# Finding the tokens of each expert block: scattered copies in DRAM, or an inverted slot list and gathers, in a two-layer Mamba and mixture-of-experts kernel

## The reference, cut to what matters

```python
xn = layernorm(x)
# layer 0: selective scan over the 256 positions of a sequence, 16 states per channel
A_bar = exp(delta * A);  Bx = delta * x * B_sel
h_t = A_bar_t * h_{t-1} + Bx_t;  y = sum_n C_n * h_n + D * x
x = x + scan(xn) + moe(xn)
xn = layernorm(x)
# layer 1: heads of 8 channels, softmax of keys and queries
tran_V = softmax(K)^T outer V, summed over the heads;  out = softmax(Q) @ tran_V
x = x + heads(xn) + layernorm_affine(xn) + moe(layernorm_affine(xn))
# moe: 8 experts, the best 2 of each token
w, i = top_k(softmax(x @ gate), 2);  out = sum_k w_k * (gelu(x @ W1[i_k] + b1) @ W2[i_k] + b2)
```

## Time and profile before

| | us |
|---|---|
| median of 3 runs | 1062.06 |
| profiled execution, own time | 1060.0 |
| its span | 1058.3 |
| routing of layer 0 done | 116.7 |
| layer 0 scan groups | 118.9 to 537.1 |
| routing of layer 1 done | 637.0 |
| layer 1 heads done | 1035.4 |

### The profile page before, as it was taken

How to read it: one execution, slowest core, us unless ns; L and a number is a source line. 1 busy time by engine, 2 the same in 40 slices (tenths; PEclk the granted TensorE clock), 3 DMA queues, 4 the chain that set the end, 5 groups by cost and what they waited for, 6 DMA issues and landing times.

```text
span 1058.3 us, 17046 instructions
## 1 busy us (share of the span) xinstructions
PE 690.6 (65%) x4452; PEld 432.3 (41%) x4452; DVE 840.0 (79%) x1702; ACT 528.6 (50%) x1217; POOL 386.3 (36%) x358
## 2 busy tenths in 40 slices
PE   1883467399888988898921543233687786869670
PEld 0331122155545554455501442122565564747450
DVE  4898999699999999989967765814776859495968
ACT  2566533258676767666503611002565667465630
POOL 1565477613131313121201546773223232323320
PEclk9856598899998989898975555766696988889785
DMA  8369911101010101010050001111011111111108
GB/s 245 99 126 160 152 53 50 52 22 42 21 41 20 39 21 39 17 36 19 27 148 23 1 0 44 45 50 38 26 34 32 33 35 30 30 35 37 33 15 238
DMA packets 80124, 58.47 MB, mean 55 GB/s; under 512 B 9922, under 2 KB 71816, under 8 KB 80036
## 3 DMA queue, kind: packets, MB, share of 16 engines
q1 hardware_dynamic: 67108, 38.42, 17.1%
q0 software_dynamic: 8704, 16.87, 5.1%
q10 hardware_dynamic: 4224, 2.10, 0.7%
HBM read 28.89 MB, written 29.50 MB: 55 GB/s over the span
## 4 chain that ended last, share of the span: by engine, by line
DVE 35%; PE 20%; POOL 13%; ACT 12%; issue 11%; DMA 8%; SPq 1%; ACTq 0%; DVEq 0%; POOLq 0%
POOL slots L425 13%; ACT decay L521 5%; DVE decay L1231 4%; DVE work L1082 4%; DMA results<-res,xrow 4%; DVE hid_l L1045 4%; PE pb L827 3%; DVE x L970 3%; DVE work L1224 3%; DMA xrow<-slots 2%; DVE work L1091 2%; PE py L709 2%; PE po L749 2%; ACT hid L533 2%; DVE res L1050 2%
## 5 line engine op out<-in xcount | busy, mean ns | idle before, releaser
L431 POOL DMA_INDIRECT results<-res,xrow x144 | 164.2, 1140 | 469.3 <-DVE res L1050 455.6
L1082 DVE TENSOR_TENSOR_SCAN work<-decay,work 128x256 f32<-128x256 f32 x256 | 162.8, 679 | 1.1
L425 POOL DMA_INDIRECT slots<-rows,slot x128 | 136.7, 1068 | 72.2 <-issue 36.0
L533 ACT ACTIVATE hid<-ph,b 128x128 f32<-128x128 f32 x432 | 123.5, 369 | 69.3 <-PE ph L734 60.4
L709 PE MATMUL py<-work,idf 128*128 128x512 f32 x256 | 141.4, 641 | 1.1 <-DVE work L1091 1.0
L525 ACT COPY xrT<-px 128x256 f16<-128x256 f16 x144 | 53.4, 371 | 150.0 <-PE px L717 149.8
L749 PE MATMUL po<-w,hid_h 128*128 x576 | 124.4, 296 | 0.0
L690 PE MATMUL pb<-parts,pick 96*128 96x512 bf16 x256 | 86.3, 419 | 45.2 <-DVE work L1091 22.9
L748 PE MATMUL po<-w,hid_l 128*128 x576 | 115.5, 235 | 0.0
L1050 DVE TENSOR_REDUCE res<-po 128x128 f32<-128x256 f32 x144 | 59.5, 413 | 67.5 <-PE po L749 67.2
L1045 DVE TENSOR_TENSOR hid_l<-hid,hid_h 128x512 f16<-128x512 f32 x144 | 98.8, 686 | 17.0 <-ACT hid_h L539 16.8
(11 more groups left out here) (189 smaller groups left out, 1428.7 us busy)
## 6 DMA issues: line engine op xcount, KB each, us to landing
slots<-xrow SPq DMA_DIRECT2D x2, 4644.0 KB, 50.3
xrow<-slots SPq DMA_DIRECT2D x144, 64.5 KB, 1.9
decay<-in_w SPq DMA_DIRECT2D x32, 256.0 KB, 3.2
decay<-results SPq DMA_DIRECT2D x16, 256.0 KB, 4.2
big<-results SPq DMA_DIRECT2D x16, 256.0 KB, 4.7
results<-res,xrow POOLq DMA_INDIRECT x144, 2.3
x<-in_x SPq DMA_DIRECT2D x4, 512.0 KB, 6.4
slots<-rows,slot POOLq DMA_INDIRECT x128, 2.4
```

The costliest lines, as they stand in the source:

```text
L425: e.indirect_dma_start(slots_dram[l], bass.IndirectOffsetOnAxis(slot[:, k, t:t + 1], 0), rows[:, t, :], None).then_inc(s_disp[l][i], 16)
L431: e.indirect_dma_start(res_dram[l], bass.IndirectOffsetOnAxis(ids_of(j % XR), 0), res[:, j % XR, :], None, bounds_check=NRES - 1, oob_is_e ...
L533: ins = e.activation(hid[:, j % 2, c * P:(c + 1) * P], hidden(l, j)[:, c * P:(c + 1) * P], ACT.Gelu, bias=b1[:, col(en * HC + (l * NE * HC ...
L1082: ins = e.tensor_tensor_scan(work[:, 2 + n % 2, sl], decay[:, n, sl], work[:, n % 2, sl], 0.0, ALU.mult, ALU.add)
```

## The change

The slots are not filled by scattering rows any more. The rows (now 512 bytes, no number in them) are written to `rows_dram` in token order, group by group, by SyncE. On chip the list "slot of each pair" is turned into "pair of each slot". For each of 64 columns of pairs, VectorE makes a one-hot row of the low 7 bits of the slot (`lows`, 128 wide), and GpSimd one of the block number, times 128 (q + 1), and the same one-hot times the row number (`high_one`, `high_row`, 72 wide). PE multiplies them, 128 matmuls into one bank, and `rows_at` makes `pair_of` (for the scatter of results) and `row_of` (for the gather). Eight chunks of eight columns, two buffers each. Then GpSimd fetches each block's rows with an indirect DMA, four blocks ahead of its sends, and sends the results as before.

In layer 0 `lows` lies in group 0's scan loop after `scan(n)` for n = 0, 1, 3, 4, 6, 7, 9, 10, `invert` on PE two ticks later, and `rows_at` and `b2_in` at n = 14. In layer 1 all of it is in a row, `lows` inside `route` ahead of the weights of the choices. Blocks: layer 0 has 0, 10, 10, 10, 10, 10, 11, 11 ticks in its groups and a drain after the last scan; layer 1 has 9 in each of its 8 groups, with two quarters of `head_sum` at tick 7 and two at tick 8, and its products at ticks 5 and 6. The tick count runs on over group borders. The experts' numbers are read into registers nine at a time, not one per block. The sums over the heads are now turned when they are scaled (`t_` is written with a stride and read without one). The buffers of the hidden layer and of the one-hots share one arena.

```diff
-BPG = BLOCKS // (GROUPS - FIRST)
-ROWF = 2 * D + 2
+TICKS = ((0, 10, 10, 10, 10, 10, 11, 11), (9,) * GROUPS)
+ROWF = 2 * D
+AHEAD = 4
+CHUNK = 8
 @@ sync
-            e.wait_ge(s_const, 1)
-            for l in range(2):
-                e.dma_start(slots_dram[l].rearrange(...), fill[:, :]...).then_inc(s_zeroed[l], 16)
-                for i in range(DISP):
-                    e.wait_ge(s_disp[l][i], 16 * 2 * TILES // DISP)
+                for g in range(GROUPS):
+                    e.wait_ge(s_rlo, l * GROUPS + g + 1)
+                    e.dma_start(rows_dram[l][g * GC:(g + 1) * GC, :].rearrange("(t p) c -> p t c", p=P),
+                                rows[:, g * TG:(g + 1) * TG, :]).then_inc(s_rout, 16)
+                e.wait_ge(s_rout, 16 * GROUPS * (l + 1))
                 e.dma_start(b2, a[f"b2_{l}"]).then_inc(s_b2, 16)
-                for g in range(FIRST + 1, GROUPS):
-                    for j in range(BPG):
-                        block_rows(g, j, True)
 @@ gpsimd, after s_slot
-                            e.indirect_dma_start(slots_dram[l], bass.IndirectOffsetOnAxis(slot[:, k, t:t + 1], 0),
-                                                 rows[:, t, :], None).then_inc(s_disp[l][i], 16)
+                for c in range(CHUNKS):
+                    if c >= 2:
+                        e.wait_ge(s_inv, l * CHUNKS + c - 1)
+                    for i in range(CHUNK):
+                        q = c * CHUNK + i
+                        ins = e.tensor_scalar(high_one[:, c % 2, i, :], count_h[:, 0:BLOCKS], at_f[:, 1, q:q + 1],
+                                              float(P * (q + 1)), ALU.is_equal, ALU.mult)
+                    st.seq(ins)
+                    e.tensor_scalar(high_row[:, c % 2, :, :]..., high_one[:, c % 2, :, :]..., 0.0, row_f[:, 0:1],
+                                    ALU.is_gt, ALU.mult).then_inc(s_high1, 1)
+                def fetch(b):
+                    at = l * BLOCKS + b
+                    if at >= XR:
+                        e.wait_ge(s_xr, at - XR + 1)
+                    e.indirect_dma_start(xrow[:, b % XR, :], None, rows_dram[l],
+                                         bass.IndirectOffsetOnAxis(row_of[:, b:b + 1], 0)).then_inc(s_row[b % XR], 16)
+                for b in range(AHEAD):
+                    fetch(b)
+                for b in range(BLOCKS):
+                    if b + AHEAD < BLOCKS:
+                        fetch(b + AHEAD)
+                    send(b)
 @@ tensor
+            def invert(l, c):
+                e.wait_ge(s_low1, l * CHUNKS + c + 1)
+                e.wait_ge(s_high1, l * CHUNKS + c + 1)
+                for i in range(CHUNK):
+                    e.matmul(po[:, 0:BLOCKS], low_one[:, c % 2, i, :], high_one[:, c % 2, i, :], ...)
+                    ins = e.matmul(po[:, 0:BLOCKS], low_one[:, c % 2, i, :], high_row[:, c % 2, i, :], ...)
+                ins.then_inc(s_inv, 1)
 @@ tensor, last group of layer 0
+                if g == GROUPS - 1:
+                    for tick in range(BLOCKS, BLOCKS + DRAIN):
+                        blocks_tick(0, tick, expert)
                     to_tokens(g)
 @@ vector
+            def lows(l, c):
+                if c >= 2:
+                    e.wait_ge(s_inv, l * CHUNKS + c - 1)
+                for i in range(CHUNK):
+                    q = c * CHUNK + i
+                    ins = e.tensor_scalar(low_one[:, c % 2, i, :], count_h[:, :], at_f[:, 0, q:q + 1], None,
+                                          ALU.is_equal)
+                ins.then_inc(s_low1, 1)
+            def rows_at(l):
+                e.wait_ge(s_inv, (l + 1) * CHUNKS)
+                ...
+                e.tensor_scalar(row_of[:, :], pair_of[:, :], NTOK - 1, None, ALU.bitwise_and).then_inc(s_idx, 1)
-                    e.tensor_tensor(t_[:, 0:TG * HD * HD].rearrange("p (c d) -> p c d", d=HD), ...)
+                    e.tensor_tensor(t_[:, 0:TG * HD * HD].rearrange("p (t c d) -> p t d c", t=TG, d=HD), ...)
-                    tt = t_[:, t * HD * HD:(t + 1) * HD * HD].rearrange("p (d c) -> p c d", d=HD)\
+                    tt = t_[:, t * HD * HD:(t + 1) * HD * HD].rearrange("p (c d) -> p c d", d=HD)\
```

More of the change, by code:

```diff
@@ L43 @@
 HR = 3
-DISP = 4
 XIN = 4
 XR = 6
-assert BLOCKS >= 2 * TILES + NE - 1 and BPG % XR == 0 and BPG + DRAIN - 1 <= NS
+AHEAD = 4
+PAIRS = 2 * TILES
+CHUNK = 8
+CHUNKS = PAIRS // CHUNK
+BATCH = 9
+assert BLOCKS >= 2 * TILES + NE - 1 and all(sum(t) == BLOCKS for t in TICKS) and BLOCKS % BATCH == 0
 class Steps:
     def __init__(self, eng, sem):
-        self.eng, self.sem, self.n, self.off = eng, sem, 0, 0
+        self.eng, self.sem, self.n = eng, sem, 0
     def done(self, ins):
@@ L66, in seq @@
         self.wait()
[L68 to L82, removed]
 def build(nc, a, out):
@@ L98, in dram @@
             return nc.dram_tensor(name, shape, dt, kind="Internal").ap()
[L101 removed]
+        rows_dram = [dram(f"rows{l}", [NTOK, ROWF], F16) for l in range(2)]
         NRES = 2 * NTOK
@@ L764, in to_tokens, with scan_group @@
                 ins.then_inc(s_yTT, 1)
-            def scan_group(g, first=False, last=False, with_blocks=True):
+            def scan_group(g, expert):
+                ticks = ticks_of(0, g)
                 for n in range(NS):
@@ L771, in scan_group @@
                         b_row(g, n + 2)
-                    elif not last:
+                    elif g + 1 < GROUPS:
                         b_row(g + 1, n + 2 - NS)
-                    if with_blocks:
-                        blocks_at(0, g, n)
+                    if g == 0:
+                        for c in range(CHUNKS):
+                            if inverted_at(c) == n:
+                                invert(0, c)
+                    if n == 0 and g == 1:
+                        e.wait_ge(s_b2p, 1)
+                    if n < len(ticks):
+                        blocks_tick(0, ticks[n], expert)
                     if n >= 2:
                         y_sum(g, n - 2)
-                    if n == 0 and not first:
+                    if n == 0 and g > 0:
                         to_tokens(g - 1)
@@ L950, in route @@
                 e.tensor_scalar(eid[:, :], hit[0:1, :], float(NE - 1), None, ALU.min).then_inc(s_slot, 1)
+                for c in range(CHUNKS if l else 0):
+                    lows(l, c)
                 e.wait_ge(s_expout, l + 1)
@@ L1108, in scan_group @@
                     scan(g, n)
-                    if with_blocks:
-                        blocks_at(0, g, n)
+                    if g == 0:
+                        for c in range(CHUNKS):
+                            if inverted_at(c) == n + 2:
+                                lows(0, c)
+                        if n == NS - 2:
+                            rows_at(0)
+                            b2_in(0)
+                    if n < len(ticks):
+                        blocks_tick(0, ticks[n])
                     if n >= 1:
                         weigh(g, n - 1)
-                    if n == 1 and not first:
+                    if n == 1 and g > 0:
                         end_scan(g - 1)
                 weigh(g, NS - 1)
-                if not last:
+                if g + 1 < GROUPS:
                     begin_scan(g + 1)
@@ L1175, in _ @@
             route(1)
+            rows_at(1)
+            b2_in(1)
             q_, k_, v_, t_, o_ = (work[:, i, :] for i in range(5))
```

388 lines of the change are left out of this document (186 added, 202 removed).

## The result

The changed kernel takes 1259.78 us (median of 4 runs, 1254.39 to 1264.63) where the kernel before takes 1062.3 on the same chip (1061.4 to 1063.25): a ratio of 1.186, interval 1.181 to 1.191. Slower was forecast, but by 16 us; it is 197. The span of the profiled execution went from 1058.3 to 1252.6 us.

| stretch | before | after | difference | forecast |
|---|---|---|---|---|
| start to `eid` of layer 0 | 116.5 | 117.2 | +0.7 | +0.6 |
| group 0 | 39.0 | 70.4 | +31.4 | +20.4 |
| groups 1 to 7 | 377.0 | 446.3 | +69.3 | +1.0 |
| end of the last scan to `combine` | 9.2 | 16.8 | +7.5 | +6.0 |
| `combine` to `eid` of layer 1 | 92.7 | 93.3 | +0.6 | 0 |

A forecast was written before the change was run, and what follows sets the result against it. VectorE bounds layer 0; in layer 1 VectorE and PE take turns. Group 0 +20.4, groups 1 to 7 +1.0, layer 0's end +6.0, layer 1 -10.7: +16.7 on 1060.0, 1076.7, stated as 1078; range 1046 to 1110.

The forecast's parts named there:

- the late rows: Block ticks: PE waits for gathered rows, 28 us in layer 0's groups 1 to 7, 2.5 us a period in layer 1.
- GpSimd's one-hots: Layer 1's inversion: 2.8 us a chunk plus 0.3; as a rival 5 us a chunk, 1097 in all, chance 0.08.
- the register reads: Path from turn to `block_split`: 0.5 us taken off because the register load is done nine at a time.
- The loop of 11.3 us per three ticks: Layer 0's ticks: row fetch through out takes 11.3 us against 9.9, losing 1.4 three times a ten-tick group.
- the path of the row: Layer 0's ticks, from the end of out through send and gather to the row's landing: 4.5 us.
- The first rival: Rows come in time: gather lands in 2.0 us or less, layer 0 loses 6 us rather than 28; 1042, chance 0.22.
- the meetings: Waits for GpSimd's small instructions: 5 us for 28 in group 0, 0.3 us a chunk in layer 1.
- Group 0's work on VectorE: Layer 0's group 0: 64 one-hots at 0.20 us, 12.8 in all, `rows_at` 0.7 and `b2_in` 1.9.
- The shared way to SBUF: Rival, VectorE's one-hots beside GpSimd: all or half wait, 0.93 us each, +40 or +20; 1098 to 1118, chance 0.12.
- The end of layer 0: The blocks' drain behind the last scan delays the load of results: +6.0 us, bounds +3 and +9.
- the rival on it: Layer 1: the turned `t_` does not make L1231 shorter, +25 us; 1103, chance 0.05.
- the period: Layer 1, one group: 43.8 us, of it 2.5 for late rows, where it was 48.4.

The follow-up runs named there:

- a_single: The changed kernel with each expert number read into a register one at a time instead of nine: 1229.92 us, ratio 1.157.
- a_all: The changed kernel with rows fetched five blocks ahead, single register reads and all one-hots on VectorE: 1032.29 us, ratio 0.976 to the kernel before.
- a_highs_dve: The changed kernel with the block-number one-hots and their row products made on VectorE, none on GpSimd: 1217.1 us, ratio 1.145.
- b_batch: The kernel before with expert numbers read into registers twelve at a time on PE and ACT: 1090.39 us, ratio 1.030.

## Why the prediction was right or wrong

The ladder from the kernel after down to the best version, in us of 1062:

| step | ratio | worth |
|---|---|---|
| kernel after | 1.186 | |
| rows in time and single reads | 1.012 | 185 |
| one-hots on VectorE | 0.976 | 38 |
| drain among the scans | 0.966 | 11, of which the profiles show 5.5 |

**The sign was right and the size was not.** 1259.78 us lies far outside 1046 to 1110. None of the rivals had the time either: the worst ended at 1118. Two of the three costs stood in the sum at a fraction of their price, the late rows and GpSimd's one-hots (these as a rival too). The third, the register reads, stood in it as a saving.

**The row loop: right mechanism, mis-sized term.** PE waits for the gather in most ticks, as forecast (97 of 144 blocks). The loop of 11.3 us per three ticks was 12.0: the part through VectorE and PE was right (6.6 for 6.8), the path of the row was 5.4 for 4.5. The forecast had taken the dispatch's spacing of 1.27 where send and gather in turn are 1.57 apart, and 2.4 to land where it took 3.0 to the turn; the page's median from issue to landing is 2.9. (Its upper bound, 2.6, was meant as the direct load's 1.9 and the time of generation; with the 0.97 of GpSimd's indirect DMA in the earlier trace rows that sum is 2.9.) The 0.7 us raise the loss of a loop from 1.4 to 2.1 us: by the forecast's own count, three losses in a group of ten ticks, some 6 us a group where it had 4. The group lost more, in a_single 10.4 us over nine steps. So besides the row's path the step that fails is PE's speed, which I took as that of the earlier trace rows for every tick. In a_single the clock is down at 0.70 and 0.73 in two of eight ticks in a row, and up to 3.5 of the 10.4 us are the lower clock's by the estimate above; with the 6 of the loop that is nearly all. It makes 82 us in layer 0's groups where I had 28. In layer 1 I gave the row wait 2.5 us a period; in the kernel after one period has waits of 3.91 and 3.48 us at a single turn each, and with single reads the wait costs 49 - 39.5 = 9.5 us a period (73 us in layer 1). In all the sum had 28 + 7 x 2.5 = 45 us for late rows, and they cost 155 with single reads. The first rival, rows in time at 1042, had "a loop of about 10.0 us" as its condition, and the loop was 12.0, so it falls. a_all comes near its time, 1032, but by other ways (rows a tick earlier, single reads, cheap one-hots).

**The register reads: the step that failed outright.** The prediction took 0.5 us off the path of each block "for the register load that is now done nine at a time", a saving. It was a pause of PE of 3.2 to 4.8 us, 16 times, with as many batches in ACT's order; in time it was 30 us with late rows and 65 with rows in time. The 0.5 us was about right for one read: a_single pauses 0.19 to 0.61 us in front of `block_up`. What I left out is that nine reads stand together in the order of an engine that others wait for, while single ones lie in gaps that the loop has anyway. No row of the kernel before showed a batch; nine times the 0.5 would have been the bound to set, and the text set none.

**GpSimd's one-hots: the rival's side, and more.** I scaled the price from a two-input instruction of 512 elements in 1.27 us and took 3.1 us a chunk, with the meetings; it was 7.25, above the rival's 5. (The 3.4 us that the text has for that instruction's rate does not come out either: 1152 elements at 1.27 us for 512 are 2.9.) By elements a one-hot of 72 would have been 72/512 of 1.27, 0.18 us, and `high_row` of 576 would have been 1.43; they take 0.57 to 0.6 and 2.2. A row of one large instruction could not show what a small one costs, nor what this other form costs. So the start of layer 1 was 41 us later than forecast (108.4 for 67.3); a_highs_dve gets 34.5 of them back. In group 0 GpSimd's eight chunks take about 61 us, and the group could not be 59.

**Group 0's work on VectorE** was about right: 64 one-hots at 0.17 us are 11 us (12.8 forecast), `rows_at` and `b2_in` took 0.6 and 1.9.
**The shared way to SBUF** cost up to 2.4 of the 5 us that I had put in for meetings. VectorE's timeline in group 0 of the kernel after has these two, the longest set of eight one-hots and one of the two longest pairs of scans:

```profile
122.84 2.19 DVE L904 TENSOR_SCALAR arena<-count_h,mask 128x128 bf16<-128x128 bf16 x8
...
152.91 1.77 DVE L1116 TENSOR_TENSOR_SCAN work<-decay,work 128x256 f32<-128x256 f32 x2
```

The other seven sets of eight one-hots take 1.38 to 1.39 us (1.36 to 1.37 in a_highs_dve). The 16 pairs of scans take 21.9 us in all, and 20.3 in the kernel before and in a_highs_dve, where no one-hots are made on GpSimd. GpSimd's chunk is 7.25 to 8.00 us beside VectorE's scans (7.67 in the mean) and 7.25 beside an idle VectorE. So the rival at 1098 to 1118, with 0.93 us for each one-hot, falls, although the time was on its side of the range. The Trainium skill, "GPSIMD Engine Reference", section "Key points", has GpSimd share interfaces with VectorE's 2-port modes and two-input instructions; the earlier trace rows showed it for large ones, and the trace agrees here too, with small numbers.

**The rest.** The end of layer 0 was +7.5 for +6.0 (bounds 3 and 9). L1231 fell to 1.22 as forecast, so the rival on it falls; but its 25 us are worth only 11 alone, and the larger part of what is missing is VectorE's longer wait for ACT's cast. With rows in time the period is 38.2 to 39.8 in a_all; the forecast had 43.8, of it 2.5 for rows, so 41.3. The 2 us are in the PE part: from the last product of a group to the first scaling of its sums it was 12.0 us on average, for 14.1.

## What to carry to other kernels

Where an engine waits in a loop for a transfer, add up the whole loop (result, queue, issue, landing, and the way back to the result) against the ticks that it spans, and give the transfer one tick more than the sum: here one number in the source, AHEAD, was worth 119 to 155 us. Instructions that are counted as nothing, such as reads into registers, have to be spread over an engine's order and not gathered in it. A small instruction on GpSimd must not be priced by scaling a large one down: measure one of its size, or leave it on VectorE, which did the 72-wide one-hots over three times as fast.

## What the runs showed of the hardware

- Nine reads of a 4-byte number from SBUF into PE's registers held PE for 3.2 to 4.8 us; single reads 0.19 to 0.61; twelve at a time, in b_batch, 3.2 to 4.4. ACT's batches of nine held it up to 4.1.
- GpSimd, 16-bit one-input instruction with a pointer scalar: 0.57 to 0.6 us for 72 elements per partition, 2.2 us for 576. VectorE does the same in 0.16 and 0.37. Side by side, GpSimd's chunk was 6% longer in the mean, VectorE's 16 pairs of scans 8%.
- A gather of 128 rows of 512 bytes lands 2.9 us (median) after its issue; send and gather in turn start 1.57 us apart, where copies of the dispatch stood 1.27 apart.
- PE's clock is at its full level, 2.4 GHz, in layer 0's groups while VectorE sets the pace (0.97 and 1.00 in the two ten-block groups shown, whose rows are in time), and it falls toward 1.2 GHz in stretches right behind idle time of 1.5 to 4.8 us: granted clock 0.70 and 0.73 over ticks that then take 4.50 and 4.30 us in place of 3.29.
- Reading 1024 f32 elements with a stride costs 0.8 us more than in order; writing 256 with a stride costs 0.2 us more.
